# Second routed layer: token-major output projection with VectorE sums into x, and low parts of the scaled x from POOL

## The chip, the cores and the metric

One core of one Trainium2 chip runs the whole program. The metric is the device time in microseconds of one execution. The core's engines are TensorE (PE in the profile, with its weight loads as PEld), VectorE (DVE), ScalarE (ACT), POOL (GpSimd) and SyncE (SP), which issues the transfers. Each works through its own queue in order and waits on semaphores that the others raise.

## What is computed

The input x is 16 batches x 256 tokens x 128 features in float32. Four layers follow one another, each a cross-attention and a feed-forward part. The change is in the feed-forward part of the third of them, which routes tokens over 16 experts. It is the second of the two routed ones whose weights are loaded and split ahead in this way. Its reference, cut down:

```
n = layernorm(x)
w = gating(n)                      # softmax over the experts chosen, [tokens, 16]
q = sum_e w[:, e] * (n @ q_proj[e])      # k and v alike
a = softmax(causal(q @ k.T / sqrt(128))) @ v
x = x + sum_e w[:, e] * (a @ o_proj[e])
```

All products are to float32 accuracy.

## The kernel before

The tokens lie in x_sb as 32 tiles of 128; a block is four tiles (512 tokens, two batches), and there are ITERS = 8 blocks. `layer2_ffn` (L1588 on) writes the work of a block out by hand for each engine in a function `main(j, q)`. `run_mains` calls it for blocks 0 and 1, in a hardware loop for blocks 2 to 5, and for blocks 6 and 7. The order in which these functions issue is the order of each queue; nothing reorders it.

A block has two parts. **The q/k/v part** has a step per expert e. A selector product (`spread`, L1799) spreads the routing weights of expert e of all 512 tokens over the 128 partitions into a PSUM bank psR; VectorE multiplies the normalised x (xT, feature-major) by it (`scale_by`, L1980) into a ring of four, xs. ScalarE rounds that to xsh (L1727); VectorE subtracts, which gives the low part xsl (`low_part`, L1984). TensorE then adds nine products of rounded operands (low weight x high x, high x low, high x high, for q, k and v) to three PSUM banks (L1865). Expert 0 has three float32 products instead (L1860). The selector of step e+2 stands ahead of the products of step e. Between the steps stand the gate of the next block (`front_gate` to `front_parts`: some thirty small VectorE operations of 64 columns, after the scalings of e = 6, 7, 8, 9, 11 and 13) and its small products (after e = 2, 4 and 14).

**The part after it** has the attention of the block (scores, exponentials, transposes, `attend`) and, for the block before, the output projection `mix_o`: 16 steps, each a selector, a scaling of the attended values aoT by the same weights, and a float32 product with wo[e] into one bank psX (L1843). ScalarE copies the feature-major sum (L1722), four transposes turn it (L1793), and VectorE adds it to x (`add`, L2005) in the q/k/v part of two blocks later. POOL keeps a copy of the routes for that (L1681). `front_ln`, `front_xn` and `front_norm` prepare the normalised x of block j+2 there.

`layer2_ffn_weights` (L1571) lists what is loaded, copied and split for the layer while the attention ahead of it (`narrow_attention`) runs. The class `Ahead` (L110) does it: SyncE starts the loads in the first block of that attention, and POOL splits wq, wk and wv into high and low parts at its end (L134, L136).

The lines that decide the pace of a step, on TensorE:

```
pe.wait_ge(s("scaled").sem, s("scaled").at(n - 1))          # in spread
pe.wait_ge(s("x_split").sem, s("x_split").at(split_no(j, e) + 1))   # ahead of the nine products
```

and on VectorE:

```
dve.wait_ge(s("gate_bcast").sem, s("gate_bcast").at(n + 1))
dve.wait_ge(s("hidden").sem, s("hidden").at(n + 1 - RING))
```

## Time and profile before

| | |
|---|---|
| median of three runs | 2017.27 us (2017.11 to 2026.06) |
| the profiled execution | 2015.44 us, its span 2013.3 us |
| TensorE busy | 1626.2 us (81%), mean granted clock 0.899 of 2.4 GHz |
| TensorE weight loads busy | 1104.1 us (55%) |
| VectorE busy | 1284.4 us (64%) |
| ScalarE busy | 926.6 us (46%) |
| POOL busy | 210.0 us (10%) |

The layer that the change is in lies between about 1058 and 1613 us of the span. Busy times of TensorE come from records whose ends are modelled and which overlap, so the distance between starts is the better measure of what a product costs. The profile's views used here are the busy time of each engine by stretch, the timeline of one engine (start, duration, line, names, and in brackets the idle time ahead of it with what ended it), and the groups of like instructions with their mean duration.

### The profile page before, as it was taken

Reading aid. Unit: us, or ns where it says so; the run is one execution under the profiler, and the core shown is the slowest. Engines: PE = TensorE matmul, PEld = TensorE weight load, DVE = VectorE, ACT = ScalarE, POOL = GpSimd, SP = SyncE. Lnnn points to the kernel's source line nnn. Section 1 sums busy time; section 2 is a strip of 40 time slices with the busy share of each in tenths; the row PEclk is TensorE's granted clock in tenths of the full one; section 3 lists DMA queues with packets and bytes.
Section 4 is the critical chain, followed back from the end, with each engine's and each line's share of the span. In section 5 each row is a group of like instructions: output and inputs, shape, how many; then the busy total and the mean of one; then the engine's idle time right before and its main releaser. Section 6 shows DMA issues by size and latency. Waiting matters only on the chain. (4 is left out here: it accounts for less than half of the span.)

```text
span 2013.3 us, 27147 instructions
## 1 busy us (share of the span) xinstructions
PE 1626.2 (81%) x8633; PEld 1104.1 (55%) x8633; DVE 1284.4 (64%) x2870; ACT 926.6 (46%) x1759; POOL 210.0 (10%) x188
## 2 busy tenths in 40 slices
PE   6999938978869999978975899999999968848004
PEld 5777726855546666645653656656666445523004
DVE  4777771147657667646765566666665548776985
ACT  3555523356635565545551322222222146626862
POOL 2110020011200000011131000000000011010320
PEclk9999967959979999979996999999999969969557
DMA  4000000032100000023210000000000012100000
GB/s 149 1 1 0 0 1 0 0 112 47 39 1 0 1 0 0 1 91 104 60 26 0 1 1 0 1 1 0 0 1 0 0 50 50 43 0 0 0 0 42
DMA packets 23456, 41.71 MB, mean 21 GB/s; under 512 B 7720, under 2 KB 11184, under 8 KB 22320
## 3 DMA queue, kind: packets, MB, share of 16 engines
q1 hardware_dynamic: 23344, 40.32, 6.8%
q8 instruction: 58, 0.95, 0.2%
q14 instruction: 54, 0.44, 0.1%
HBM read 19.32 MB, written 2.10 MB: 11 GB/s over the span
## 5 line engine op out<-in xcount | busy, mean ns | idle before, releaser
L962 DVE TENSOR_REDUCE mP_a<-psY_a 128x8 f32<-128x512 f32 x192 | 128.2, 688 | 118.8 <-PE psY_a L800 117.9
L720 ACT ACTIVATE probs_a<-psX_a 128x512 f32<-128x512 f32 x192 | 109.1, 595 | 149.0 <-PE psX_a L827 148.3
L1727 ACT ACTIVATE xsh_f<-xs_f 128x512 fp32r<-128x512 f32 x120 | 75.8, 632 | 202.8 <-DVE xs_f L1980 202.6
L1980 DVE TENSOR_TENSOR xs_f<-xT_f,psR_f 128x512 f32<-128x512 f32 x128 | 86.9, 686 | 83.1 <-PE psR_f L1799 75.3
L1843 PE MATMUL psX_f<-xs_f,wo_f2w 128*128 128x512 f32 x256 | 128.6, 594 | 0.0
L2375 PE MATMUL ps_f<-wT_f,xq_f 128*128 128x128 f32 x192 | 24.5, 292 | 125.4 <-DVE xq_f L2396 125.4
L1980 DVE TENSOR_TENSOR xs_f<-aoT_f,psR_f 128x512 f32<-128x512 f32 x128 | 85.8, 685 | 61.6 <-PE psR_f L1799 61.4
L1507 DVE SCALAR_TENSOR_TENSOR g_f<-psU_f,cols_f1w,t_f 128x512 f32<-128x512 f32 (+1 forms) x104 | 77.9, 749 | 73.2 <-ACT t_f L1320 71.0
L800 PE MATMUL psY_a<-ks_a,xs_a 96*128 96x256 f32 x384 | 100.7, 367 | 28.0 <-DMA xs_a<-ql_a 16.3
L1402 PE MATMUL psO_f<-h_f,w_f1w 128*128 128x512 f32 (+1 forms) x208 | 107.6, 599 | 0.0
L1320 ACT ACTIVATE t_f<-psU_f,cols_f1w 128x512 f32<-128x512 f32 (+1 forms) x104 | 71.2, 684 | 76.0 <-PE psU_f L1386 76.0
L800 PEld LDWEIGHTS psY_a<-ks_a,xs_a 96*128 96x128 f32 x384 | 69.0, 215 | 59.6 <-issue 20.9
L827 PE MATMUL psX_a<-xs_a,ks_a 128*128 128x256 f32 x384 | 89.9, 336 | 10.2 <-ACT xs_a L712 10.2
L2375 PEld LDWEIGHTS ps_f<-wT_f,xq_f 128*128 128x128 f32 x192 | 23.8, 206 | 126.7 <-issue 126.7
L969 DVE RECIPROCAL heads_a<-psV_a 128x256 f32<-128x256 f32 x48 | 84.0, 1749 | 13.8 <-PE psV_a L840 13.8
L1984 DVE TENSOR_TENSOR xsl_f<-xs_f,xsh_f 128x512 fp32r<-128x512 f32 x120 | 82.5, 688 | 1.1
L827 PEld LDWEIGHTS psX_a<-xs_a,ks_a 128*128 128x128 f32 x384 | 66.8, 206 | 27.1 <-ACT xs_a L712 21.8
L1514 DVE TENSOR_TENSOR h_f<-act_h_f,psR_f 128x512 f32<-128x512 f32 (+1 forms) x104 | 70.5, 678 | 13.4 <-ACT act_h_f L1326 8.5
L179 POOL TENSOR_TENSOR rstd_f<-vareps_f,mhalf 128x4 f32<-128x4 f32 x16 | 16.2, 1010 | 580.1 <-DVE vareps_f L165 580.1
L376 ACT ACTIVATE vhat_a<-psF_a 64x256 f32<-64x256 f32 x122 | 46.1, 378 | 61.9 <-PE psF_a L434 61.1
L1865 PE MATMUL psQ_f<-xsh_f,wql_f2w 128*128 128x512 f32 x120 | 66.4, 554 | 5.0 <-DVE xsl_f L1984 4.9
L507 DVE TENSOR_REDUCE smax_a<-psS_a 128x16 f32<-128x1024 f32 x32 | 39.2, 1224 | 47.9 <-PE psS_a L441 47.9
(434 smaller groups left out, 4320.2 us busy)
## 6 DMA issues: line engine op xcount, KB each, us to landing
xs_a<-qh_a SPq DMA_DIRECT2D x192, 64.0 KB, 2.0
xs_a<-ql_a SPq DMA_DIRECT2D x96, 64.0 KB, 2.0
x_sb<-in_x SPq DMA_DIRECT2D x1, 2048.0 KB, 8.5
out<-x_sb SPq DMA_DIRECT2D x1, 2048.0 KB, 6.3
w_f1w<-in_F_w SPq DMA_DIRECT2D x2, 792.0 KB
ctxT<-in_ctxT SPq DMA_DIRECT2D x1, 1024.0 KB, 12.3
maskf_a<-in_mask SPq DMA_DIRECT2D x8, 128.0 KB, 2.3
maskf_a<-in_maskT SPq DMA_DIRECT2D x8, 128.0 KB, 2.5
```

The costliest lines, as they stand in the source:

```text
L720: nc.scalar.activation(probs[:, b % 2, g, :, :], psX[g % 2][:].rearrange("p (e t) -> p e t", e=2), ACT.Exp, scale=float(dv) ** -0.5).then_ ...
L800: ins = nc.tensor.matmul(psY[h % 2][:, e * GK:(e + 1) * GK], xs[0:MAXROW, j % 2, g, t:t + P], ks[0:MAXROW, j % 2, p, g, :], start=not mask ...
L827: ins = nc.tensor.matmul(psX[g % 2][:, e * ST:(e + 1) * ST], ks[:, j % 2, p, g, e * P:(e + 1) * P], xs[:, j % 2, g, p * ST:(p + 1) * ST], ...
L962: nc.vector.tensor_reduce(mP[:, b % 2, h // 2, col:col + 8], psY[h % 2][:].rearrange("p (h k) -> p h k", h=8), axis=AX.X, op=ALU.max).then ...
L969: nc.vector.reciprocal(heads[:, b % 2, :], psV[:, ST:2 * ST]).then_inc(s("sums_inverted").sem, 1)
L1320: nc.scalar.activation(t3[r, g % 2, :], psU[g % 2][r, 1, :], ACT.Identity, bias=cols[r, CH + g % CH:CH + g % CH + 1])\
L1402: ins = nc.tensor.matmul(psO[:], w2[0:rows[k], k, :], h[0:rows[k], g % 2, :], start=False, stop=k == CH - 1)
L1507: nc.vector.scalar_tensor_tensor(g_[r, g % 2, :], psU[g % 2][r, 0, :], cols[r, k:k + 1], t3[r, g % 2, :], ALU.add, ALU.mult).then_inc(s("h ...
L1727: nc.scalar.activation(xsh[:, e % RING, :], xs[:, e % RING, :], ACT.Copy).then_inc(s("x_high").sem, 1)
L1843: nc.tensor.matmul(psX[:], wo[:, e, :], xs[:, e % RING, :], start=e == 0, stop=e == E - 1)\
L1980: nc.vector.tensor_tensor(xs[:, e % RING, :], src, psR[e % 2][:], ALU.mult).then_inc(s("scaled").sem, 1)
L1984: nc.vector.tensor_tensor(xsl[:, e % RING, :], xs[:, e % RING, :], xsh[:, e % RING, :], ALU.subtract)\
```

## The change

**Output projection.** Instead of scaling the attended values by each expert's weights and adding in PSUM, the kernel multiplies the unscaled attended values, tokens as the stationary side, by the output weights of four experts at once: one group k of a block is tile c = k // 4 and experts 4g to 4g+3 with g = k % 4, 512 columns, in three rounded products (high and low halves aoh, aol of the attended values, and woh, wol of the weights). 16 groups a block alternate between two PSUM banks psO. VectorE adds the four results of a group to x, each times its column of the routing weights (`add_o`). Eight of the groups of block j-1 are multiplied in the q/k/v part of block j, after the steps 1, 3, ... 15; the other eight stand among the attention's products after it. The second selector product, the copies and the transposes go. The attended values' low half is made by VectorE (`attended_low`), which also keeps a copy of the routes.

**Low parts on POOL.** xsl comes from POOL, for all 16 experts; expert 0 has nine rounded products too.

**Smaller.** The selector of expert e is one column read 128 times, so that its table is 16 columns instead of 2048. The weights wq and wk are loaded into two raw buffers, split by POOL in the fifth block of the attention, and the buffers are then refilled with wv and wo (SyncE, in the seventh block), which POOL splits at the end; the first routed layer's split moves to the middle too. The score banks of the attention are packed in three banks instead of four, in the order 0, 2, 1, 3.

```diff
@@ class Ahead @@
+    def refill(self, pr, sp):
+        for k, pair in enumerate(self.refills):
+            sp.wait_ge(pr.sig("split").sem, pr.sig("split").at(2 * k + 2))
+            load(sp, pr.sig("refilled"), [pair])
...
-            pr.nc.gpsimd.tensor_tensor(lo, raw, hi, ALU.subtract)
+            pr.nc.gpsimd.tensor_tensor(lo, raw, hi, ALU.subtract).then_inc(pr.sig("split").sem, 1)
@@ narrow_attention @@
+                if j == ITERS - 2:
+                    ahead.refill(pr, sp)
...
-            ahead.split(pr, pool)
+                if j == ITERS // 2:
+                    ahead.split(pr, pool, 0)
+            ahead.split(pr, pool, 1)
@@ layer2_ffn, gpsimd @@
-            def keep_routes(j, q):
...
+            def low_part(j, e):
+                pool.wait_ge(s("x_high").sem, s("x_high").at(qn(j, e) + 1))
+                nc.gpsimd.tensor_tensor(xsl[:, e % RING, :], xs[:, e % RING, :], xsh[:, e % RING, :], ALU.subtract)\
+                    .then_inc(s("x_split").sem, 1)
             def main(j, q):
+                for e in range(E):
+                    low_part(j, e)
                 if has_second_next(j):
                     front(j + 2)
-                keep_routes(j, q)
@@ layer2_ffn, scalar @@
-                nc.scalar.activation(aoT[:, q, :], psM[:], ACT.Copy).then_inc(s("ao_ready").sem, 1)
+                if not is_first(j, 2):
+                    act.wait_ge(s("o_part").sem, s("o_part").at(OSTEPS * (j - 1)))
+                nc.scalar.activation(aoh[:, q, :], psM[:], ACT.Copy).then_inc(s("ao_high").sem, 1)
@@ layer2_ffn, tensor @@
-                nc.tensor.matmul(psR[e % 2][:], selb[:, e * P:(e + 1) * P], weights, start=True, stop=True)\
+                nc.tensor.matmul(psR[e % 2][:], selb[:, e:e + 1].broadcast_to([P, P]), weights, start=True, stop=True)\
...
+            def mix_o(j, q, k):
+                c, g = k // 4, k % 4
+                pe.wait_ge(s("o_steps").sem, s("o_steps").at(4 * (OSTEPS * j + k - 1)))
+                for m, (left, right) in enumerate(((aol, woh), (aoh, wol), (aoh, woh))):
+                    ins = nc.tensor.matmul(psO[k % 2][:], left[:, q, c * P:(c + 1) * P], right[:, 4 * g:4 * g + 4, :], start=m == 0, stop=m == 2)
+                ins.then_inc(s("o_part").sem, 1)
...
-                    if e == 10 and not is_first(j, 2):
-                        if not is_last(j):
-                            pe.wait_ge(s("gate_exp").sem, s("gate_exp").at(2 * j + 3))
-                        out_T(j - 2)
+                    if not is_first(j, 1) and e % 2 == 1:
+                        mix_o(j - 1, 1 - q, e // 2)
...
+                some_o(IN_LOOP, 10)
+                scores(j)
+                v_to_tokens(j)
+                some_o(10, 13)
+                probs_T(j, 0)
+                probs_T(j, 1)
+                some_o(13, 15)
+                probs_T(j, 2)
+                probs_T(j, 3)
+                some_o(15, OSTEPS)
+                attend(j)
@@ layer2_ffn, vector @@
+            def attended_low(j, q):
+                dve.wait_ge(s("ao_high").sem, s("ao_high").at(j + 1))
+                nc.vector.tensor_tensor(aol[:, q, :], psM[:], aoh[:, q, :], ALU.subtract).then_inc(s("ao_ready").sem, 1)
...
+            def add_o(j, k):
+                c, g = k // 4, k % 4
+                xc = x_sb[:, bass.ds(j * TPI + c, 1), :].rearrange("p a d -> p (a d)")
+                dve.wait_ge(s("routes_kept").sem, s("routes_kept").at(j + 1))
+                dve.wait_ge(s("o_part").sem, s("o_part").at(OSTEPS * j + k + 1))
+                for m in range(4):
+                    e = 4 * g + m
+                    dve.wait_ge(s("o_steps").sem, s("o_steps").at(4 * (OSTEPS * j + k) + m))
+                    nc.vector.scalar_tensor_tensor(xc, psO[k % 2][:, m * P:(m + 1) * P], routes_o[:, c, e:e + 1], xc, ALU.mult, ALU.add)\
+                        .then_inc(s("o_steps").sem, 1)
             def main(j, q):
                 for e in range(E):
                     scale_by(qn(j, e), e, xT[:, q, :])
-                    if e > 1:
-                        low_part(j, e - 1)
-                    if e == 12 and not is_first(j, 2):
-                        add(j - 2)
+                    if not is_first(j, 1) and e % 2 == 0 and e:
+                        add_o(j - 1, e // 2 - 1)
...
+                some_o(IN_LOOP - 1, 10)
+                maxima(j)
+                some_o(10, 11)
+                normalise(j, 0)
+                normalise(j, 1)
+                some_o(11, 12)
+                normalise(j, 2)
+                normalise(j, 3)
+                some_o(12, 14)
                 if has_second_next(j):
-                    stages.update({10: lambda: front_ln(j + 2), 12: lambda: front_xn(j + 2), 14: lambda: front_norm(j + 2)})
...
+                    front_ln(j + 2)
+                some_o(14, OSTEPS)
+                if has_second_next(j):
+                    front_xn(j + 2)
+                    front_norm(j + 2)
+                attended_low(j, q)
+                keep_routes(j, q)
```

How the change orders VectorE's queue at the start of a q/k/v part that carries sums (block 1). First the kernel before, in the same place of block 0, whose order there is that of all its blocks: L1980 scales, L1984 makes low parts, L1941 on is the gate.

```order
L1935 TENSOR_SCALAR ssq_f<-ssq_f 128x4
L1980 TENSOR_TENSOR xs_f<-xT_f,psR_f 128x512 x3
L1984 TENSOR_TENSOR xsl_f<-xs_f,xsh_f 128x512
L1980 TENSOR_TENSOR xs_f<-xT_f,psR_f 128x512
L1984 TENSOR_TENSOR xsl_f<-xs_f,xsh_f 128x512
L1980 TENSOR_TENSOR xs_f<-xT_f,psR_f 128x512
L1984 TENSOR_TENSOR xsl_f<-xs_f,xsh_f 128x512
L1980 TENSOR_TENSOR xs_f<-xT_f,psR_f 128x512
```

Now the change, block 1 (L1965 scales, L1999 is the sum of `add_o`, L1985 the attended values' low half):

```order
L1920 TENSOR_SCALAR ssq_f<-ssq_f 128x4
L1985 TENSOR_TENSOR aol_f<-psM_f,aoh_f 128x512
L1989 COPY routes_o_f<-routes_f 128x64
L1965 TENSOR_TENSOR xs_f<-xT_f,psR_f 128x512 x3
L1999 SCALAR_TENSOR_TENSOR x_sb<-psO_f,routes_o_f,x_sb 128x128 x4
L1965 TENSOR_TENSOR xs_f<-xT_f,psR_f 128x512 x2
L1999 SCALAR_TENSOR_TENSOR x_sb<-psO_f,routes_o_f,x_sb 128x128 x4
L1965 TENSOR_TENSOR xs_f<-xT_f,psR_f 128x512 x2
L1999 SCALAR_TENSOR_TENSOR x_sb<-psO_f,routes_o_f,x_sb 128x128 x4
L1926 TENSOR_TENSOR lg_f<-psM_f,rn_f 128x64
```

The low parts are gone from this queue; four sums stand after the scaling of every even expert from 2 on and ahead of that of the odd one behind it.

On TensorE, steps 1 and 2 of the same block in the change (L1849 the nine products, L1832 the output group, L1792 the selector):

```order
L1849 MATMUL psQ_f<-xsl_f,wvh_f2w 128x512
L1849 MATMUL psQ_f<-xsh_f,wvh_f2w 128x512
L1832 MATMUL psO_f<-woh_f2w,aol_f 128x512
L1832 MATMUL psO_f<-wol_f2w,aoh_f 128x512
L1832 MATMUL psO_f<-woh_f2w,aoh_f 128x512
L1792 MATMUL psR_f<-rwTb_f,selb_f2w 128x512
L1849 MATMUL psQ_f<-xsh_f,wql_f2w 128x512
L1849 MATMUL psQ_f<-xsl_f,wqh_f2w 128x512
```

The output group stands behind the products of the odd step and ahead of the selector and the products of the even one.

## Rows read from the trace of the kernel before

**Rows 1.** Busy by stretch: start:end, length, PE, PEld, DVE, ACT, POOL, PEclk, DMA, GB/s.

```profile
1080.00:1613.00 533.00, 503.02 (x2056) 325.51 (x2056) 329.31 (x792) 145.74 (x342) 23.11 (x22) 0.98 0.00 1
1270.20:1311.20 41.00, 40.13 (x176) 29.34 (x177) 25.66 (x62) 10.82 (x18) 0.00 (x0) 1.00 0.00 1
1311.20:1331.00 19.80, 18.88 (x76) 9.96 (x76) 14.81 (x41) 6.80 (x24) 1.01 (x1) 1.00 0.00 1
```

**Rows 2.** Timeline of TensorE, a steady block: start, us, instruction, idle before.

```profile
1268.98 0.59 PE L1799 MATMUL psR_f<-rwTb_f,selb_f2w 128*128 128x512 bf16 x2
1270.46 1.07 PE L1860 MATMUL psQ_f<-xs_f,wq_f2w 128*128 128x512 f32 x2
1273.08 0.38 PE L1799 MATMUL psR_f<-rwTb_f,selb_f2w 128*128 128x512 bf16 x1
1275.40 0.39 PE L1799 MATMUL psR_f<-rwTb_f,selb_f2w 128*128 128x512 bf16 x1
1311.17 0.61 PE L1799 MATMUL psR_f<-rwTo_f,selb_f2w 128*128 128x512 bf16 x2
1333.83 0.59 PE L1799 MATMUL psR_f<-rwTb_f,selb_f2w 128*128 128x512 bf16 x2
```

**Rows 3.** Timeline of TensorE: two output steps.

```profile
1329.97 0.38 PE L1799 MATMUL psR_f<-rwTo_f,selb_f2w 128*128 128x512 bf16 x1
1331.04 0.38 PE L1799 MATMUL psR_f<-rwTo_f,selb_f2w 128*128 128x512 bf16 x1
```

**Rows 4.** Timeline of VectorE, the same block.

```profile
1273.59 0.69 DVE L1980 TENSOR_TENSOR xs_f<-xT_f,psR_f 128x512 f32<-128x512 f32 x1 [1.42 <-PE psR_f L1799]
1283.81 0.23 DVE L1941 TENSOR_TENSOR lg_f<-psM_f,rn_f 128x64 f32<-128x64 f32 x1 [1.53 <-PE psM_f L1780]
1288.41 0.22 DVE L1951 TENSOR_REDUCE top_f<-gated_f 128x4 f32<-128x64 f32 x1
1289.12 0.22 DVE L1035 TENSOR_REDUCE gs_f<-lg_f 128x4 f32<-128x64 f32 x1
1289.37 0.22 DVE L1036 TENSOR_TENSOR tmp_f<-lg_f,gs_f 128x64 f32<-128x64 f32 x1
1290.58 0.69 DVE L1980 TENSOR_TENSOR xs_f<-xT_f,psR_f 128x512 f32<-128x512 f32 x1 [0.21 <-DVE oh_f L1039]
```

**Rows 5.** Timelines of VectorE and ScalarE: one scaling and its rounding.

```profile
1300.50 0.68 DVE L1980 TENSOR_TENSOR xs_f<-xT_f,psR_f 128x512 f32<-128x512 f32 x1
1301.21 0.63 ACT L1727 ACTIVATE xsh_f<-xs_f 128x512 fp32r<-128x512 f32 x1 [2.49 <-DVE xs_f L1980]
```

**Rows 6.** Groups by line: count | busy us, mean ns | idle before.

```profile
L2401 DVE SCALAR_TENSOR_TENSOR x_sb<-ps_f,scale_f,x_sb 128x512 f32 x6 | 4.5, 751 | 5.0 <-PE ps_f L2375 4.8
L533 DVE TENSOR_TENSOR x_sb<-x_sb,psC_a 128x128 f32<-128x128 f32 x16 | 4.5, 283 | 7.8 <-PE psC_a L456 7.7
L2005 DVE TENSOR_TENSOR x_sb<-x_sb,psM_f 128x512 f32<-128x512 f32 x4 | 2.8, 688 | 9.3 <-PE psM_f L1793 9.3
L331 POOL TENSOR_TENSOR cbl_a<-cb_a,cbh_a 128x256 fp32r<-128x256 f32 x8 | 5.9, 740 | 1.2 <-POOL cbh_a L328 0.2
L136 POOL TENSOR_TENSOR wkl_f2w<-wk_f2w,wkh_f2w 128x2048 fp32r<-128x2048 f32 x1 | 4.6, 4629 | 0.1
```

**Rows 7.** Timeline of VectorE, preparing the block after next.

```profile
1328.93 1.11 DVE L171 TENSOR_SCALAR xn_f<-x_sb,mean_f,rstd_f 128x128 f32 x4
1331.38 0.17 DVE L1935 TENSOR_SCALAR ssq_f<-ssq_f 128x4 f32<-128x4 f32 x1 [0.15 <-ACT sq_f L1701]
```

**Rows 8.** Busy time by stretch, start of the second block (columns as rows 1).

```profile
1139.00:1145.00 6.00, 5.92 (x9) 2.56 (x10) 2.09 (x4) 1.26 (x2) 1.65 (x2) 0.51 0.01 3
```

**Rows 9.** Timeline of TensorE in the attention before.

```profile
916.18 0.61 PE L794 MATMUL psY_a<-maskb_a,identb 128*128 128x512 bf16 x1 [4.63 <-DMA xs_a<-ql_a]
```

**Rows 10.** Timeline of VectorE, first scaling and last sum of the layer.

```profile
1083.47 2.08 DVE L1980 TENSOR_TENSOR xs_f<-xT_f,psR_f 128x512 f32<-128x512 f32 x3
1612.09 0.69 DVE L2005 TENSOR_TENSOR x_sb<-x_sb,psM_f 128x512 f32<-128x512 f32 x1 [3.36 <-PE psM_f L1793]
```

More of the change, by code:

```diff
@@ L1636, in qn @@
         def qn(j, e):
[L1637 to L1644 removed]
+            return E * j + e
         def run_mains(eng, main):
@@ L1968, in front_weights, with front_parts @@
                 steps.done(nc.vector.reciprocal(gs[:], gs[:]))
[L1969 to L1972 removed]
+                steps.done(nc.vector.tensor_tensor(routes[:, q, :, :], ex[:], gs[:].unsqueeze(2).broadcast_to(g4), ALU.mult))
+            def front_parts(steps, q):
+                three_parts(nc, steps, routes[:, q, :, :], parts[:], hi[:], rest[:], mid[:], E).then_inc(s("gate_ready").sem, 1)
                 steps.n += 2
```

244 lines of the change are left out of this document (93 added, 151 removed).

## Prediction

> **What bounds the kernel now.** I read the busy time by stretches first. In the second routed layer (1080 to 1613 us of the span) TensorE is nearly always at work: 40.13 of 41.00 us in the part of a block that makes q, k and v, 18.88 of 19.80 in the part after it [rows 1]; VectorE has 25.66 and 14.81 us there. The TensorE timeline of one steady block gives the beats [rows 2]: the q/k/v part begins at 1270.46, is over at 1311.17 (40.7 us), and the next block's selectors follow at 1333.83. Block to block is 1268.98 to 1333.83, 64.85 us. One expert's step is 2.32 us (1273.08 to 1275.40: one selector matmul and nine products, 0.23 us each). In the second part an output step costs 1.07 us [rows 3]. So TensorE bounds this layer, and VectorE runs up to two steps ahead of it. That lead is what hides the path of an expert's step: scale on VectorE, round on ScalarE, low part, products.
>
> **What the change takes off TensorE.** Per block: 16 output steps of 1.07 us become 16 groups of three rounded products, 3 x 0.23 = 0.70 us each, -5.9 us; the transposes back of the output go (about 0.4, half of a float32 product below); three float32 products of the first step (1270.46 to 1273.08, 2.6 us [rows 2]) become nine rounded ones, 2.1 us. Together -6.9 us per block, 55 us in eight. It counts only where TensorE still ends the wait.
>
> **What it adds, part by part.**
> *Sums.* A block gets 64 VectorE sums of 128x128, PSUM times a column plus x. The same form with 512 columns took 751 ns; a column costs (688 - 283) / 384 = 1.05 ns [rows 6], so 128 columns take about 0.35 us. Each waits on the one before it. Chained operations of 0.22 us start 0.25 us apart (1289.12 and 1289.37 [rows 4]), 0.035 after the end of the one before, so a chained sum comes every 0.386 us. Unchained ones overlap: four normalisations of 0.34 us take 1.11 together, one per 0.26 [rows 7]. A group of four followed by an unchained operation is 3 x 0.386 + 0.26 = 1.42 us, a group followed by another group 1.54. Bounds for one sum: 0.26 (no price for the chain) and, in the four looped blocks, the 0.21 us of register work seen before the scaling at 1290.58 [rows 4] once per group, +13 us in all.
> *Low part on POOL.* It took 740 ns for 256 columns and 4629 for 2048 [rows 6]: 2.17 ns a column, 1.30 us for 512. Bounds 1.11 (slope alone) and 1.48 (twice 256). Against 2.32 us per step POOL keeps up; its rate costs nothing, its latency does.
> *The wait that decides.* VectorE's queue in a q/k/v part is now: scale(e), the four sums of group e/2 - 1 for even e, scale(e+1). That group's product stands on TensorE behind the nine products of step e-1. So the sums can't start before TensorE is at step e, and scale(e+1) queues behind them: the lead of two steps is gone. From the start of step e's products: the group's last product started 0.47 us earlier, and a VectorE operation starts 0.51 us after its producer starts (1273.08 to 1273.59 [rows 2, 4]), so 0.04; sums 1.42; scale to round 0.71 (1300.50 to 1301.21 [rows 5]); round 0.63 + 0.05; low part 1.30 + 0.04. That is 4.19 us until step e+1 can start, where 2.32 are needed: **TensorE stands 1.87 us at each of seven odd steps**. Step 7 waits 0.74 longer, for four small gate operations between the sums and its scaling (the first 0.23 at 1283.81, the others taken at 0.17 like the small one of [rows 7]), and step 9 waits 2.17 longer, for the second-best search (1288.41 to 1290.58 [rows 4]). The small transposes and gate products of the part vanish in these stalls. Its length: 16 x 2.1 + 13 selectors x 0.23 = 36.6, seven groups of products 4.9, stalls 13.1 + 2.9 = **57.5 us where 40.7 stood**, +16.8. The last block has no gate work, +13.9. Seven blocks carry sums (the first has none): 6 x 16.8 + 13.9 = +114.7.
> *After the q/k/v part* two PSUM banks alternate, so products follow VectorE. VectorE: 0.95 until group 7 is there, nine groups x 1.54 = 13.9, its other work 5.2 (the 14.81 us of 41 operations less 15 scalings at 0.64, where some adjoin [rows 1]), the wait for the squares 1.35 (from the normalisation at 1328.93 to 1331.38, less its own 1.11 [rows 7]), low half and copy of the routes 0.8, and then a full hand-off to the next block's first step, 2.8: 25.0 us, against 1311.17 to the first product of the next block, 24.1. Five times +1.0; block 6 has nothing to prepare for a block 8, -4.1 on VectorE, which TensorE before couldn't use: -3.2. Sum +1.8.
> *The ends.* The first block starts 1.6 us later (hand-off) and pays low half, copy and hand-off again at its end: +3 net of its cheaper first step. The last block: 18.3 us to the low half, then sixteen groups x 1.54 = 24.7 and 1.0 to the first, 44.0, against 1311.17's counterpart to the last sum, 44.9: -1.
> *The clock.* After idle TensorE is granted 1.2 GHz: about half the clock over the 6 us with which the second block begins [rows 8], some 5.5 us of them work, costing half of that. Steady blocks had none of it. Now TensorE stands about 8 us before every block (its last product waits for nothing more than VectorE's long queue), +2.7 us x 6 (the first restart was there before), and 4 us before step 9; I take 1.5 us there, six times. With the last block's half share: +25. Bounds: 0, and the whole layer at the low level (a rival).
> *Covered or small.* Weight splits on POOL now sit in the middle and at the end of the attention before; the subtraction alone is 4.63 us each [rows 6]. POOL has nothing else to do in those stretches but the next statistics, which are needed half a tile group later; with that cover gone each split would cost its own time. In that attention 3 MB less are loaded while the mask is fetched; TensorE stood 4.63 us there for a transfer [rows 9]: -5. A selector now is one column read 128 times; no row has such a load. Below nothing; above one product, 0.23 x 128 x half of the steps (the others stand anyway) = +15. I take nothing, since a plain selector load hides.
>
> **Sum:** 3 + 114.7 + 1.8 - 1 + 25 - 5 = +139 us on this layer's 529.3 (1083.47 to the last sum's end at 1612.78 [rows 10]). The profiled execution took 2015.44 us (span 2013.3): 2154. The median of the three runs shown is 1.8 us above it, so **2156 us, 7% slower**.
>
> **A rule against the price of the chain.** The rows say that a chained operation costs 0.13 us more than an unchained one [rows 4, 7]. The Trainium skill (VectorE: DVE Perf Modes, The DRAIN you can't avoid) says that a semaphore after each operation costs nothing extra, eight copies having taken 13.88 us either way. By that rule the sum comes 58 us lower, as worked out under rival 2; the rows decide for me.
>
> **Rivals.**
> 1. *TensorE's saving wins* (faster). Place: odd steps of the q/k/v part. -6.9 us x 8 and -5 of the attention: **1957**. It decides where a stall is under 6.9 / 7 = 1.0 us, so where the next scaled x is ready 3.3 us after the sums can begin. Of these the hand-off without any sum takes 2.73, so four sums would have to fit in 0.6 us; four of the cheapest operations of that size take 1.04. For it: VectorE is busy only 25.66 of 41.00 us [rows 1]. Against: the order of its queue, which no average shows. 5%.
> 2. *Chained sums cost what unchained ones do.* 147 chained sums inside the q/k/v parts and 316 after them, 463 x 0.126 = 58 us less: **2098**. For it: nothing but that the chained pair seen is of small operations. 10%.
> 3. *The clock stays at 1.2 GHz.* A pair of steps has 23 products; at 0.43 us each it is 9.8 instead of 7.2 us, 18 us per block, if in most blocks: **2260**. For it: the gaps of 1.9 us in every 7.2; against: a slow TensorE has no gaps, and the second block, which begins slow [rows 8], ran at full clock after it: the layer's mean is 0.98 [rows 1]. 6%.
> 4. *The change doesn't do what it says* (the order of the queues differs in the looped blocks, no stall, no gain): **2017**. The printed order shows all blocks alike. 2%.
>
> **How the numbers follow.** My forecast has 77%. Its own terms (sum price -58, POOL -11/+10, registers +13, selector +15, clock -25/+30) seldom all fall on one side. The range, 2090 to 2220, takes in rival 2 and leaves out rivals 1, 3, 4 (13%) and a rest. About 0.5% (10 us) is what a measurement of this kernel can tell from no change. Faster: rival 1, 5%. Same: rival 4 and a coincidence, 3%. Slower: 92%.
>
> **What would show it.** Right: 512 sums with a mean of 0.35 us; 128 low parts on POOL of about 1.3 us; TensorE idle before the products of odd steps some 1.9 us, released by POOL; a steady block of about 86 us; VectorE idle for the output product just before the sums at even steps; clock near 0.9 over the layer. Wrong: no wait of products on POOL's low part; sums starting while TensorE is a step behind; blocks near 58 us; the attention before it longer than now.

## The result and the profile after

| | before | changed |
|---|---|---|
| median | 2017.66 us (4 runs, 2017.11 to 2026.06) | 2202.45 us (4 runs, 2194.59 to 2206.09) |
| ratio | | 1.0900, 95% interval 1.0859 to 1.0941 |
| profiled execution, span | 2015.44, 2013.3 us | 2194.59, 2192.6 us |
| first product to last sum of the layer | 1084.62 to 1612.78, 528.2 us | 1091.39 to 1787.61, 696.2 us |
| what follows the layer | 400.5 us | 405.0 us |

The change makes the kernel 9.0% slower; the forecast was 2156 us in a range of 2090 to 2220. From the profile page of the changed kernel, its busy line and three groups (count | busy us, mean ns of one | idle time before them and what ended it):

```profile
PE 1639.4 (75%) x8575; PEld 1149.7 (52%) x8625; DVE 1324.5 (60%) x3142; ACT 920.5 (42%) x1759; POOL 369.5 (17%) x310
...
L1999 DVE SCALAR_TENSOR_TENSOR x_sb<-psO_f,routes_o_f,x_sb 128x128 f32<-128x128 f32 (+1 forms) x512 | 179.4, 350 | 291.3 <-PE psO_f L1832 214.3
...
L1690 POOL TENSOR_TENSOR xsl_f<-xs_f,xsh_f 128x512 fp32r<-128x512 f32 x128 | 162.0, 1277 | 343.5 <-ACT xsh_f L1728 343.5
...
L1849 PE MATMUL psQ_f<-xsh_f,wql_f2w 128*128 128x512 f32 x128 | 73.8, 576 | 89.7 <-POOL xsl_f L1690 89.7
```

Both new prices are as forecast: a sum 0.350 us, a low part 1.28. VectorE stood 214 us for the output products, and TensorE stood 89.7 us for POOL's low parts, which is the wait that was to show. By stretches (columns as in [rows 1]): the layer, the q/k/v part of the fourth block and the part after it (the one beside which the hardware loop returns, 3 us longer than the others), and the two parts of the last block, which has no gate work:

```profile
1088.50:1787.70 699.20, 514.26 (x2017) 369.24 (x2046) 358.05 (x1060) 140.01 (x333) 175.10 (x141) 0.90 0.00 1
1325.80:1390.90 65.10, 51.17 (x192) 37.42 (x196) 25.67 (x72) 9.27 (x17) 19.03 (x16) 0.89 0.00 1
1390.90:1419.00 28.10, 15.19 (x63) 10.72 (x63) 20.43 (x68) 8.38 (x28) 3.21 (x3) 0.80 0.01 1
1684.90:1740.80 55.90, 43.71 (x177) 31.42 (x180) 17.56 (x41) 8.00 (x13) 18.74 (x15) 1.00 0.00 0
1740.80:1787.60 46.80, 30.85 (x110) 19.05 (x108) 38.19 (x114) 5.59 (x17) 0.00 (x0) 0.89 0.00 1
```

In [rows 1] TensorE worked 40.13 of 41.00 us and VectorE 25.66. Now VectorE does the same work in that part (25.67) and TensorE somewhat more (51.17: output groups are new in it, and some of it runs at the lower clock), but in 65.1 us. Neither is the bound: they wait for each other. The TensorE timeline of that block shows where (the first product of steps 2, 3, 4, 7, 8, 9 and 10, and the selectors ahead of 7 and 9):

```profile
1333.62 0.58 PE L1849 MATMUL psQ_f<-xsh_f,wql_f2w 128*128 128x512 f32 x1
1338.15 0.49 PE L1849 MATMUL psQ_f<-xsh_f,wql_f2w 128*128 128x512 f32 x1 [1.42 <-POOL xsl_f L1690]
1341.08 0.59 PE L1849 MATMUL psQ_f<-xsh_f,wql_f2w 128*128 128x512 f32 x1
...
1351.61 0.39 PE L1792 MATMUL psR_f<-rwTb_f,selb_f2w 128*128 128x512 bf16 x1 [0.70 <-DVE xs_f L1965]
1353.61 0.49 PE L1849 MATMUL psQ_f<-xsh_f,wql_f2w 128*128 128x512 f32 x1 [1.61 <-POOL xsl_f L1690]
1356.62 0.51 PE L1849 MATMUL psQ_f<-xsh_f,wql_f2w 128*128 128x512 f32 x1
1361.14 0.39 PE L1792 MATMUL psR_f<-rwTb_f,selb_f2w 128*128 128x512 bf16 x1 [2.14 <-DVE xs_f L1965]
1363.15 0.80 PE L1849 MATMUL psQ_f<-xsh_f,wql_f2w 128*128 128x512 f32 x1 [1.61 <-POOL xsl_f L1690]
1368.53 0.72 PE L1849 MATMUL psQ_f<-xsh_f,wql_f2w 128*128 128x512 f32 x1
```

Steps 2 to 3 are 4.53 us apart, 3 to 4 are 2.93. The hand-off between the first two can be read link by link from VectorE, ScalarE and POOL:

```profile
1333.99 1.51 DVE L1999 SCALAR_TENSOR_TENSOR x_sb<-psO_f,routes_o_f,x_sb 128x128 f32 x4 [8.90 <-PE psO_f L1832]
1335.41 1.27 DVE L1965 TENSOR_TENSOR xs_f<-xT_f,psR_f 128x512 f32<-128x512 f32 x2
...
1341.36 1.51 DVE L1999 SCALAR_TENSOR_TENSOR x_sb<-psO_f,routes_o_f,x_sb 128x128 f32 x4 [4.67 <-PE psO_f L1832]
```

```profile
1336.13 1.22 ACT L1728 ACTIVATE xsh_f<-xs_f 128x512 fp32r<-128x512 f32 x2 [10.38 <-DVE xs_f L1965]
```

```profile
1336.83 2.51 POOL L1690 TENSOR_TENSOR xsl_f<-xs_f,xsh_f 128x512 fp32r<-128x512 f32 x2 [8.52 <-ACT xsh_f L1728]
```

From the first product of step 2: sums after 0.37, scaling 1.42 later, rounding 0.72, low part 0.70, products 1.32: 4.53 us. VectorE was idle for 4.67 us ahead of the next sums. It had time, but its next instruction was one that TensorE could not yet release.

### The profile page after: what moved, and what is told of

The parts are those of the page before. It is cut to its first block and busy times, and to the rows that moved or that the text cites. A ratio compares the mean times of both kernels' runs of the same rounds, so it can differ in the third digit from the quotient of the medians.

```text
span 2192.6 us, 27697 instructions
## 1 busy us (share of the span) xinstructions
PE 1639.4 (75%) x8575; PEld 1149.7 (52%) x8625; DVE 1324.5 (60%) x3142; ACT 920.5 (42%) x1759; POOL 369.5 (17%) x310
## 5 line engine op out<-in xcount | busy, mean ns | idle before, releaser
L1999 DVE SCALAR_TENSOR_TENSOR x_sb<-psO_f,routes_o_f,x_sb 128x128 f32<-128x128 f32 (+1 forms) x512 | 179.4, 350 | 291.3 <-PE psO_f L1832 214.3
L1690 POOL TENSOR_TENSOR xsl_f<-xs_f,xsh_f 128x512 fp32r<-128x512 f32 x128 | 162.0, 1277 | 343.5 <-ACT xsh_f L1728 343.5
L1849 PE MATMUL psQ_f<-xsh_f,wql_f2w 128*128 128x512 f32 x128 | 73.8, 576 | 89.7 <-POOL xsl_f L1690 89.7
L2370 PE MATMUL ps_f<-wT_f,xq_f 128*128 128x128 f32 x192 | 24.8, 295 | 126.7 <-DVE xq_f L2391 126.7
L1965 DVE TENSOR_TENSOR xs_f<-xT_f,psR_f 128x512 f32<-128x512 f32 x128 | 84.9, 681 | 20.8 <-PE psR_f L1792 13.8
L1832 PE MATMUL psO_f<-woh_f2w,aol_f 128*128 128x512 f32 x128 | 63.3, 495 | 40.2 <-DVE x_sb L1999 38.5
L1849 PEld LDWEIGHTS psQ_f<-xsh_f,wql_f2w 128*128 128x128 f32 x128 | 27.4, 214 | 106.8 <-POOL xsl_f L1690 98.5
L1792 PE MATMUL psR_f<-rwTb_f,selb_f2w 128*128 128x512 bf16 x98 | 41.5, 424 | 53.7 <-DVE xs_f L1965 52.0
```

The lines of the kernel that those rows point to most:

```text
L1690: nc.gpsimd.tensor_tensor(xsl[:, e % RING, :], xs[:, e % RING, :], xsh[:, e % RING, :], ALU.subtract)\
L1849: ins = nc.tensor.matmul(psQKV[n][:], wp[:, e, :], xp[:, r, :], start=e == 0 and m == 0, stop=e == E - 1 and m == 2)
L1965: nc.vector.tensor_tensor(xs[:, e % RING, :], src, psR[e % 2][:], ALU.mult).then_inc(s("scaled").sem, 1)
L1999: nc.vector.scalar_tensor_tensor(xc, psO[k % 2][:, m * P:(m + 1) * P], routes_o[:, c, e:e + 1], xc, ALU.mult, ALU.add)\
```

## Experiments

All kernels are variants of the changed one. "Layer" is from the first product of its first step to the end of its last sum, in the profiled execution.

| kernel | median us | starts at | layer us |
|---|---|---|---|
| before | 2017 to 2020 | 1084.6 | 528.2 |
| changed | 2202.5 | 1091.4 | 696.2 |
| sums_behind | 2078.6 | 1094.6 | 582.6 |
| lows_on_dve | 2304.9 | 1096.0 | 801.7 |
| behind_lows_dve | 2110.4 | 1096.0 | 614.0 |
| sums_free (one run) | 2136.7 | 1097.5 | 636.8 |
| splits_apart (one run) | 2192.5 | 1088.4 | 699.5 |
| warm | 2179.0 | 1102.4 | 676.4 |
| early_scales | 2071.7 | 1099.1 | 570.5 |
| more_in_loop | 2047.7 | 1096.7 | 541.5 |
| low_half_first | 2011.9 | 1086.1 | 524.9 |
| x_later | 2013.0 | 1084.8 | 523.2 |
| thirteen_in_loop | 2011.8 | 1084.3 | 521.2 |

### The sums behind the next scaling

```diff
-                    if not is_first(j, 1) and e % 2 == 0 and e:
+                    if not is_first(j, 1) and e % 2 == 1 and e > 1:
                         add_o(j - 1, e // 2 - 1)
```

Only the place of the sums in VectorE's queue moves, by one scaling.

> One thing moves against the changed kernel (2202 us): on VectorE the four sums of group k stand behind the scaling of expert 2k+3, no longer ahead of it. Queue theory (the sums wait for a product on TensorE and hold back the next scaling): the next scaling that queues behind the sums is that of step 2k+4, which is needed only after two whole steps, 5.3 us; its hand-off is 4.4 us, so TensorE no longer stands at plain odd steps, and only the gate's searches leave 1 to 2 us a block. The part that makes q, k and v falls from 65 to about 44 us in six blocks and from 56 to 39 in the last: some 140 us less, about 2060. The part after it stays at 25 us. Rival A (POOL's low parts set the pace, 1.28 us each behind the rounding): the stalls stay, released by POOL, and the time stays within 2 per cent of 2200. Rival B (half of the loss is TensorE's slow clock in whatever order): the stalls go but the granted clock stays near 0.88, about 2110.

Measured: 2078.60 us, ratio to before 1.0306 (1.0264 to 1.0348), 124 us less than the change. Steps 2 to 5 of the last block in this kernel, TensorE and then VectorE:

```profile
1595.43 0.58 PE L1849 MATMUL psQ_f<-xsh_f,wql_f2w 128*128 128x512 f32 x1
1597.76 0.58 PE L1849 MATMUL psQ_f<-xsh_f,wql_f2w 128*128 128x512 f32 x1
1600.79 0.58 PE L1849 MATMUL psQ_f<-xsh_f,wql_f2w 128*128 128x512 f32 x1
1603.11 0.58 PE L1849 MATMUL psQ_f<-xsh_f,wql_f2w 128*128 128x512 f32 x1
```

```profile
1601.00 1.51 DVE L1999 SCALAR_TENSOR_TENSOR x_sb<-psO_f,routes_o_f,x_sb 128x128 f32<-128x128 f32 x4 [2.16 <-PE psO_f L1832]
1602.43 0.68 DVE L1965 TENSOR_TENSOR xs_f<-xT_f,psR_f 128x512 f32<-128x512 f32 x1
```

The same sums wait for the same product (0.21 us after step 4 starts), but the scaling behind them at 1602.43 is that of step 6, not of step 5. A pair of steps takes 5.36 us, which is TensorE's own work, instead of 7.32. The last q/k/v part went from 55.9 to 41.7 us, a steady one from about 65 to 48. What is left above the expected 44 in a steady one is the gate's searches and slow products behind the 25 us tail; the last one has neither, so the expected 39 was less than TensorE's own work. POOL's rate as the limit (rival A) is out, and so is rival B: the granted clock of a steady q/k/v part rose from 0.89 to 0.96, and the time is 31 us below its 2110.

### Low parts on VectorE, with the sums ahead and with the sums behind

```diff
-                for e in range(E):
-                    low_part(j, e)
...
                 for e in range(E):
                     scale_by(qn(j, e), e, xT[:, q, :])
+                    if e:
+                        low_part(j, e - 1)
```

(The removed lines are POOL's; low_part(j, E - 1) follows VectorE's loop.)

> The changed kernel (2202 us) with the 128 low parts back on VectorE, each behind the next scaling as in the kernel before; the sums keep their place ahead of the odd scalings. Queue theory: the hand-off at an odd step is sums 1.43, scaling 0.6, the next scaling 0.6 (which hides the rounding), low part 0.7 where POOL took 1.28: 4.38 becomes about 3.9 to 4.0 us, so 0.4 x 7 x 7 = 20 us less, and VectorE operations are no longer stretched to over 1 us beside a POOL one: 2175 to 2185. Rival (moving the low parts to POOL is what lost the time): well under 2100, most of the stalls gone. Rival on the other side (VectorE is short of time): slower than 2210, since VectorE gets 11 us of work more in each block and the low part of step e can only follow the next scaling.

Measured: 2304.88 us, 1.1428 (1.1391 to 1.1465). My number was 125 us off, and the rival on the other side came true: I had looked at odd steps alone. TensorE, first products of steps 10, 11 and 12 of the fourth block, and VectorE ahead of step 10:

```profile
1413.98 0.50 PE L1842 MATMUL psQ_f<-xsh_f,wql_f2w 128*128 128x512 f32 x1 [2.87 <-DVE xsl_f L1962]
1417.36 0.98 PE L1842 MATMUL psQ_f<-xsh_f,wql_f2w 128*128 128x512 f32 x1
1423.92 0.50 PE L1842 MATMUL psQ_f<-xsh_f,wql_f2w 128*128 128x512 f32 x1 [2.75 <-DVE xsl_f L1962]
```

```profile
1411.22 1.51 DVE L1997 SCALAR_TENSOR_TENSOR x_sb<-psO_f,routes_o_f,x_sb 128x128 f32 x4 [5.61 <-PE psO_f L1825]
1412.65 0.68 DVE L1958 TENSOR_TENSOR xs_f<-xT_f,psR_f 128x512 f32<-128x512 f32 x1
1413.24 0.69 DVE L1962 TENSOR_TENSOR xsl_f<-xs_f,xsh_f 128x512 fp32r<-128x512 f32 x1
```

The low part of the even step 10 (1413.24) stands behind the sums, and these wait for the group that TensorE multiplies just ahead of step 10. So the even step has no lead at all: sums 1.43, scaling 0.6, low part 0.7, TensorE idle for 2.87. This pair takes 9.9 us. With the sums in this place, having the low parts on POOL thus saves 102 us of stall. Whether they are worth as much in the better order:

> The kernel with the sums behind the next scaling (2079 us) with the low parts on VectorE, each behind the next scaling. Tells what POOL's low parts are worth once the sums stand well. Queue theory: the low part of step 2k+3 now stands behind the sums of group k, which can't start before step 2k+2: ready 0.37 + 1.43 + 0.6 + 0.7 = 3.1 us after that start, where the step is due 2.3 us after it: 0.8 us of stall per pair and 2 to 3 us at the searches: 2125 to 2150. Rival A (the order alone mattered): within 10 us of 2079. Rival B (POOL's low parts are always worth the 100 us that they were worth with the sums ahead): about 2180.

Measured: 2110.42 us, 1.0465 (1.0435 to 1.0495); 32 us above the same order with POOL, a little under my range, and far from either rival. In the last block, every other step waits 0.29 us for the low part and a pair takes 5.91 us (1631.91 to 1637.82) instead of 5.36:

```profile
1631.91 0.50 PE L1842 MATMUL psQ_f<-xsh_f,wql_f2w 128*128 128x512 f32 x1 [0.29 <-DVE xsl_f L1962]
1634.85 0.59 PE L1842 MATMUL psQ_f<-xsh_f,wql_f2w 128*128 128x512 f32 x1
```

The two parts of the change don't add: POOL's low parts are worth 102 us with the sums in the bad place and 32 with them in a better one.

### What a chained sum costs

```diff
-                    dve.wait_ge(s("o_steps").sem, s("o_steps").at(4 * (OSTEPS * j + k) + m))
-                    nc.vector.scalar_tensor_tensor(xc, psO[k % 2][:, m * P:(m + 1) * P], routes_o[:, c, e:e + 1], xc, ALU.mult, ALU.add)\
+                    dve.wait_ge(s("o_steps").sem, s("o_steps").at(4 * (OSTEPS * j + k) + m - 3))
+                    nc.vector.scalar_tensor_tensor(acc[:, m, :], psO[k % 2][:, m * P:(m + 1) * P], routes_o[:, c, e:e + 1], xc, ALU.mult, ALU.add)\
```

This kernel leaves out the update of x by the layer's output projection.

> The 512 sums go into four scratch tiles of 128 columns, one for each expert of a group, and none waits for the one just ahead of it (only for the one four back), so x isn't updated by this layer's output projection; the waits for the group's product and all places in the queue stay. Measures the price of the chain. My price (0.387 apart chained, 0.26 unchained): four sums take 1.13 instead of 1.51 us; 0.38 x 7 x 7 in the part that makes q, k and v, 0.5 x 9 x 8 in the parts after it: 50 to 55 us less, about 2145. Rule theory (a semaphore on the one ahead costs nothing, the spacing is that of the operation): the spacing stays at 0.387 and the time within 5 us of the changed kernel.

Measured, in one run: 2136.72 us against the 2194.59 of the changed kernel's profiled execution, 58 less; the layer alone 59.4 less. By its steps some 50 of these are the chain's: 4.00 instead of 4.38 us at a plain odd step (19 us in 49 of them), 3.1 to 4.2 us in each of six gaps between q/k/v parts, 10.6 at the end of the last block. The other 9 came with fewer slow products. Four sums and the scalings behind them:

```profile
1415.57 1.13 DVE L2000 SCALAR_TENSOR_TENSOR acc_f<-psO_f,routes_o_f,x_sb 128x128 f32<-128x128 f32 x4 [4.67 <-PE psO_f L1833]
1416.62 1.27 DVE L1966 TENSOR_TENSOR xs_f<-xT_f,psR_f 128x512 f32<-128x512 f32 x2
```

Four unchained sums take 1.13 us, one every (1.13 - 0.35) / 3 = 0.26; chained they took 1.51, one every 0.387. The prediction had 0.26 and 0.386, from other operations of [rows 4, 7]. The rule of the Trainium skill (VectorE: DVE Perf Modes, The DRAIN you can't avoid), by which a semaphore after each operation costs nothing, doesn't hold for these 128-column sums: a wait on the one just ahead costs 0.13 us each. The run takes away that wait and the dependence on its result together (each of four sums has a tile of its own), so it doesn't tell one from the other.

### POOL's splits in two tile groups

```diff
-                if j == ITERS // 2:
-                    ahead.split(pr, pool, 0)
+                if j in (ITERS // 2 - 1, ITERS // 2):
+                    ahead.split(pr, pool, 0, j - ITERS // 2 + 1)
```

(Each call splits one of the two weights.) In the changed kernel, the attention before the layer has this on POOL, and this wait on TensorE:

```profile
942.71 1.28 POOL L676 TENSOR_TENSOR x_sb<-x_sb,bo_a2w 128x512 f32<-128x512 f32 x1 [10.22 <-DVE xn_a L184]
943.93 1.89 POOL L147 CAST wqh_f2w<-raw_f2w 128x2048 fp32r<-128x2048 f32 x1
945.90 4.55 POOL L149 TENSOR_TENSOR wql_f2w<-raw_f2w,wqh_f2w 128x2048 fp32r<-128x2048 f32 x1
950.40 1.89 POOL L147 CAST wkh_f2w<-raw_f2w 128x2048 fp32r<-128x2048 f32 x1
952.36 4.49 POOL L149 TENSOR_TENSOR wkl_f2w<-raw_f2w,wkh_f2w 128x2048 fp32r<-128x2048 f32 x1
957.22 1.14 POOL L192 TENSOR_TENSOR rstd_a<-vareps_a,mhalf 128x4 f32<-128x4 f32 x1 [0.36 <-DVE vareps_a L178]
```

```profile
957.75 0.59 PE L811 MATMUL psY_a<-maskb_a,identb 128*128 128x512 bf16 x1 [6.67 <-DVE maskb_a L952]
```

Four operations, 12.9 us, stand ahead of the statistics that VectorE needs for the next tile group.

> In the attention ahead of the layer POOL makes the two weight splits after the fourth and after the fifth tile group, one each (6.4 us), instead of both after the fifth (12.9 us). Cover theory: the space between POOL's bias addition and the next statistics is about 6.3 us, so both hide but for 0.2 us, TensorE's wait of 6.67 us near 957 us falls to 1.3, and the layer starts 5 us earlier; the whole is 5 us shorter (2190 against 2195 of the profiled execution). Rival (the transfers or the scores in three banks delay that attention): the layer starts where it does now, 1088.5 us, and the wait only moves.

Measured: the wait is gone, and the statistics follow on time:

```profile
952.37 0.38 PE L812 MATMUL psY_a<-maskb_a,identb 128*128 128x512 bf16 x1 [1.29 <-DVE maskb_a L953]
```

By its first product the layer started at 1088.4, 3.0 us earlier and not 5. (The 1088.5 of the expected text is where the changed kernel's stretch above begins, ahead of its first product at 1091.4.) The three tile groups from 931.88 on took 20.5 us each at a granted clock of 0.92; in the kernel before they took 18.9 at 1.00. The other kernels bear out the split: from POOL's first instruction of that attention to the layer's first product, the eight kernels with both splits together took 216.9 to 220.5 us, the four with the splits apart 209.5 to 214.2, and the kernel before 209.4. A single run of 2192.5 us can't show 5 us in the whole.

### TensorE kept at work in its stalls

```diff
+            def warm(n, q, fresh=False):
+                for _ in range(n):
+                    nc.tensor.matmul(psQKV[0][:], zero[:], rwTb[:, q, :], start=fresh, stop=fresh)
...
+                    warm(16, q, True)
...
+                        warm(2 if e not in (7, 9) else 4 if e == 7 else 10, q)
...
+                        warm(6, q)
```

> The changed kernel (2202 us) with TensorE kept at work in its stalls: products of a zero tile that add nothing (16 ahead of the second selector of a block, 2 to 10 ahead of the selector in an odd step from 3 on, 6 ahead of the nine products of these). The order of all else, and so every stall, stays. Clock theory (about 5 us of each of six blocks are products at 1.2 GHz after a stall: steps 1, 2 and 10 took 4.1, 3.6 and 5.4 us where the last block has 2.2, 3.0 and 2.9): the granted clock of the steady blocks rises from 0.88 to 1.00 and the time falls by 25 to 35 us, to about 2172; the queue alone then accounts for the rest. Rival A (the slow stretches lie beside VectorE's waits and cost nothing): clock 1.00, time within 8 us of 2202. Rival B (the added products come late and delay the real ones): slower than 2210.

Measured: 2179.03 us, 1.0784 (1.0759 to 1.0808), 23 us less (25 to 35 were expected), with 82 more products in a block and every real instruction in its place. The fifth block's two parts, in the changed kernel and then in this one:

```profile
1419.10:1485.00 65.90, 52.17 (x192) 37.83 (x196) 25.49 (x72) 9.35 (x17) 18.91 (x15) 0.89 0.00 0
1485.00:1509.90 24.90, 14.92 (x63) 10.55 (x63) 20.30 (x68) 8.72 (x28) 3.30 (x4) 0.84 0.00 0
```

```profile
1418.40:1481.10 62.70, 61.82 (x261) 41.10 (x262) 25.49 (x72) 9.24 (x16) 19.00 (x15) 0.95 0.00 0
1481.10:1506.00 24.90, 16.10 (x81) 10.26 (x79) 20.28 (x68) 8.62 (x28) 3.25 (x3) 1.00 0.00 0
```

The clock is worth 3.2 us in this q/k/v part (2.3 to 5.7 in the others) and nothing in the part after it, which VectorE sets: 24.9 us at a clock of 0.84 and of 1.00. Summed over the second to the seventh block the gain is 21 us; the clock was not at 1.00 throughout and the added products can themselves delay a step, so this is a lower bound for what the low clock costs, beside the forecast's 25.

### Towards a version that keeps the saving

Each of these kernels holds the edits of the ones ahead of it, sums_behind's first; only the main lines are shown. The first two scalings of the next block, with their rounding and low parts, move ahead of the end of the tail (the part after q/k/v):

```diff
+                if not is_last(j):
+                    spread(qn(j + 1, 0), 0, rwTb[:, 1 - q, :])
+                    spread(qn(j + 1, 1), 1, rwTb[:, 1 - q, :])
                 some_o(15, OSTEPS)
                 attend(j)
...
+                next_scale(0)
                 some_o(13, 14)
                 if has_second_next(j):
                     front_ln(j + 2)
+                next_scale(1)
```

> The kernel with the sums behind the next scaling (2079 us), and besides the scalings of experts 0 and 1 of the next block, with their rounding and low parts, moved ahead of the last sums, of the normalised x and of the attended values' low half; their selectors stand ahead of the last output group. Theory: the 7 us in which TensorE stands ahead of a block are VectorE's queue plus one full hand-off; with the first two steps ready only VectorE's work from the last sum on is hidden behind two steps of products: 6 to 7 us less in each of seven blocks, and the slow clock of steps 0 and 1 (2.5 us a block) goes with it: about 60 us less, 2015 to 2025, level with the kernel before. Rival (VectorE is short of time over the whole block, 47 of 73 us busy, so the work only moves): the stall comes back at steps 2 to 4, and less than 25 us are won.

Measured: 2071.66 us, 1.0254 (1.0227 to 1.0281), 7 us less than sums_behind, not 60: the rival's size, with the stall a little earlier than it said. The gap between the parts fell from 25 to 21 us, but steps 0 and 1 grew, since TensorE then stood behind step 0 (2.8 and 4.0 us in two blocks) for the attended values' low half, still the second last instruction of VectorE's tail.

Then eleven groups in the first part, and the gate one to two steps earlier (PROD lists the steps behind which a group stands; a group's sums stand two scalings later):

```diff
-        IN_LOOP = 8
+        PROD = (1, 3, 5, 7, 9, 10, 11, 12, 13, 14, 15)
+        IN_LOOP = len(PROD)
```

> As the kernel with early scalings, but eleven of the sixteen output groups stand in the part that makes q, k and v (behind steps 1, 3, 5, 7, 9, 10, 11, 12, 13, 14, 15), their sums two scalings later, and the gate's pieces come one to two steps earlier, so that no pair of steps has more than one search beside its sums. Theory: with five groups instead of eight in the tail, VectorE's part of it is 4.6 us shorter, and TensorE has 2.1 us more in the first part: 2.5 us less per block in the tail and 3 us less of gate stalls in steps 8 to 10: 58 to 61 us a block against 64.85 before the change, 1975 to 1995 in all, faster than both kernels. Rival (sums every step starve the scalings): stalls at steps 11 to 15 released by POOL, and the time is above that of the kernel with early scalings.

Measured: 2047.69 us, 1.0141 (1.0119 to 1.0163). 24 us less, but the blocks took 65.1 to 69.4 us, above the expected 58 to 61. Steps 11 to 15 came every 3.03 us without a stall, so the sums don't starve the scalings; what was left was 3.9 us behind step 0 for the low half and 1.2 in step 7.

```diff
-                some_o(14, OSTEPS)
+                some_o(14, 15)
+                attended_low(j, q)
+                some_o(15, OSTEPS)
                 if has_second_next(j):
                     front_xn(j + 2)
                     front_norm(j + 2)
-                attended_low(j, q)
```

> As the kernel with eleven groups in the first part (2048 us), and: the attended values' low half ahead of the last sums and of the normalised x, the first two normalisations ahead of a group of sums, the group behind step 5 moved behind step 6 and that of 7 behind 8, and POOL's two splits of the attention before in different tile groups. Theory: TensorE's wait of 3.9 us behind step 0 (for that low half, behind seven VectorE operations) and of 1.2 us in step 7 go, and 1 to 2 us of the tail: 68.4 us a block become about 62.5, 6 us in six or seven blocks, and 3 to 5 us in the attention: 2005 to 2012, some 0.5 per cent faster than the kernel before or level with it. Rival (VectorE, 46 of 68 us busy, is the bound through its waits): the stall moves to steps 2 to 4 and under 15 us are won.

Measured: 2011.90 us (12 runs, 2006.55 to 2018.11), 0.9976 (0.9961 to 0.9990): as expected, and the first that isn't slower than before. Several edits went in at once, so the 36 us that it gained are not shown to be the low half's. In the profiled executions 10.7 us are the earlier start of the layer (the weight splits are apart now, and 2.5 us come from ahead of that attention), and 16.6 are the layer's.

Two more: one has the transposes of the next normalised x, the first pieces of the gate and the wait for the low half a step later and the groups in other places, the other thirteen groups besides.

> As the kernel with the low half first (2012 us, 64.6 us a block), with the transposes of the next block's normalised x behind step 1 instead of step 0, the gate's first three pieces one step later, the wait for the attended values' low half behind step 1, and the eleven groups behind steps 1, 2, 3, 7, 8 and 10 to 15. Theory: TensorE's wait of 1.6 to 2.1 us behind step 0 (for a normalised x that VectorE makes last in the tail) and the slow products that follow it go, and the searches stand where no sums do: 61 to 62 us a block, 3 us in seven blocks, 1985 to 1995, over 1 per cent faster than the kernel before. Rival (VectorE's waits only move): above 2005.

> The same with thirteen groups in the first part (behind steps 1, 2, 3 and 6 to 15) and three in the tail. Theory: the tail's waits for a free bank (three of 0.5 to 1.1 us a block, ended by sums) go, and TensorE has 1.4 us more in the first part and 1.4 less in the tail: 1 to 2 us a block less than with eleven, 1975 to 1990. Rival (VectorE at steps 8 to 13 has 2.1 us of scaling and sums plus the gate's 1.1 against TensorE's 3.0): stalls released by POOL appear there and it is no faster than with eleven.

Measured: 2012.97 us, 0.9990 (0.9972 to 1.0009), and 2011.75 us, 0.9971 (0.9956 to 0.9986). The expected 20 to 30 us didn't come: the stall moved from step 0 to step 2, which is x_later's rival. Thirteen groups made the layer 2.0 us shorter than eleven, in one profiled execution each; the medians can't be told apart. TensorE and VectorE at the start of a block of the last kernel:

```profile
1400.40 0.39 PE L1809 MATMUL psR_f<-rwTb_f,selb_f2w 128*128 128x512 bf16 x1 [1.36 <-DVE xs_f L1986]
1402.40 0.79 PE L1863 MATMUL psQ_f<-xsh_f,wql_f2w 128*128 128x512 f32 x1 [1.61 <-POOL xsl_f L1695]
```

```profile
1396.89 1.11 DVE L185 TENSOR_SCALAR xn_f<-x_sb,mean_f,rstd_f 128x128 f32 x4
1399.35 0.17 DVE L1941 TENSOR_SCALAR ssq_f<-ssq_f 128x4 f32<-128x4 f32 x1 [1.34 <-ACT sq_f L1719]
1399.45 0.20 DVE L2010 COPY routes_o_f<-routes_f 128x64 f32<-128x64 f32 x1
1399.65 1.28 DVE L1986 TENSOR_TENSOR xs_f<-xT_f,psR_f 128x512 f32<-128x512 f32 x2
```

The scaling of step 2 (1399.65) stands behind the normalisation and a wait of 1.34 us for ScalarE's squares. It is the same fault for the third time; moving that scaling ahead of them wasn't tried. thirteen_in_loop's layer is 7.0 us shorter than before's (521.2 against 528.2), and its whole profiled execution 6.0: what stands ahead of the layer and behind it takes nearly the same (1084.3 and 401.8 us against 1084.6 and 400.5).

## Why the prediction was right, and where it was short

The side, the mechanism and its place were right: +139 us forecast, +179 measured in the profiled executions (185 between the medians). Four of the five terms came out above the forecast and the fifth about level; the prediction had held it rare that its terms all err to one side, and its range was just wide enough. By the terms of the sum:

| | forecast | measured |
|---|---|---|
| up to the first step's products | -5 + 1.6 | +6.8 |
| first block | +1.4 | +1.0 |
| blocks 1 to 6, clock included | +128 | +146.8 |
| last block | +13 | +20.3 |
| behind the layer | 0 | +4.5 |

**The wait that decides.** Forecast 4.19 us for the hand-off, measured 4.53 beside step 2 of a steady block and 4.38 in the last one, whose pairs take 7.32 us with the clock at 1.00. All links were within 0.03 but the first: the sums start 0.22 (last block) to 0.37 us (step 2 of the steady one) after the step's first product, where I had 0.04. I had put the group's last product 0.47 us ahead of the step's first, two spacings of a product; the selector between them starts 0.04 us ahead of the product, and the distance is 0.28 (1333.34 to 1333.62). Beside step 2 the sums also started 0.65 us behind that last product, not 0.51 (0.54 beside step 4). By the whole hand-off, 4.38 to 4.53 for 4.19, seven times in seven blocks that is 9 to 17 us. The sums_behind run shows that this queue position, not POOL's rate, is the bulk of the loss (124 of 185 us).

**The gate's two long steps** were right: 0.77 more at step 7 (forecast 0.74) and 2.15 at step 9 (2.17), from 5.15 and 6.53 against 4.38 us.

**The clock.** Right in kind and nearly in size. Behind the two long waits of the steady block shown (ahead of step 0 and of step 9) TensorE was granted 1.2 GHz: products 0.43 us apart from 1363.74 to 1368.01, so that step 9 to 10 took 5.38 us where the last block has 2.93. Mean 0.90 over the layer. The fourth, sixth and seventh block are like that. In the second, third and fifth the low clock also came behind step 7's wait, and steps 7 to 8 and 9 to 10 took 4.5 us each; in two of them it came behind step 11's wait of 1.6 us as well. Against the last block's steps a block lost 4.5 to 6.5 us, where the forecast had 4.2; of these the restarts beside the gate, costed at 1.5, took 2.4 to 4.6. Blocks took 88 to 93 us (the seventh 85), about 86 being the forecast.

**The part after q/k/v.** 24.8 to 25.2 us between the parts, forecast 25.0. One gap, where the hardware loop returns, was 28.3 (before it was 25.6 against 24.0), which no term had. Behind the seventh block it was 22.1, where the forecast comes to 20.9.

**The last block** was mis-sized by its baseline: I took 40.7 us for its q/k/v part before, but without gate products that part took 37.7. Its measured length of 55.9 was forecast at 54.6. Its end took 46.8 us for 44.0.

**The attention before it** is the step that failed. The prediction said of the weight splits that "POOL has nothing else to do in those stretches but the next statistics, which are needed half a tile group later", and gave the relief of a transfer, -5. The relief came (4.63 us of [rows 9] became 1.6), but two splits are 12.9 us of POOL, where it had been idle for 7.9 ahead of those statistics: they came late, and TensorE stood 6.67 us instead of 1.29. The condition was named and its length not added up (two subtractions of 4.6 and two casts of 1.9). splits_apart removed that wait. Its 5.4 us more are a part of the 10.2 us that this line of the table is off. The tile group with the wait had a granted clock of 0.84 and the next one 0.87, and together they took 9.2 us more than two groups in the kernel before (25.87 and 21.16 against 18.9 each).

**Rivals.** The saving on TensorE (rival 1) can be seen in its piece, a group of 0.69 us (1332.89 to 1333.58) for an output step of 1.07, but it was small beside the waits: of 55 us forecast for eight blocks, the best of the later kernels shows 7.0 in its layer. Rival 2 gave 58 us for unchained sums, and sums_free measured 58, so the row of [rows 4] was the right one to choose; that the two numbers are the same is in part luck, since some 9 us of the measured ones are the clock's. Rival 3: in the q/k/v parts the clock fell only behind waits of 1.6 us and more, and not behind each of those, and it came back within about a dozen products.

## What to carry to other kernels

In an in-order queue the place of an instruction that waits matters more than its length: before putting one in, name what is queued behind it and how many steps ahead of need that is; groups of four sums, 1.4 us each, cost 124 us one place too early. An offload to another engine has no price of its own: the same low parts on POOL were worth 102 us in one order and 32 in another. Where a long job is slipped into an idle stretch, add up the whole job against that stretch, and look at what the next small instruction on that engine is for.

## What the hardware showed that was not expected

**VectorE held beside POOL.** In the changed kernel one or two 128x64 operations of a block, most of them with two SBUF inputs, take five times their time (0.22 us otherwise):

```profile
1352.49 1.15 DVE L1056 TENSOR_TENSOR oh_f<-desc_f2w,gs_f 128x64 f32<-128x64 f32 x1
```

```profile
1352.30 1.26 POOL L1690 TENSOR_TENSOR xsl_f<-xs_f,xsh_f 128x512 fp32r<-128x512 f32 x1 [5.59 <-ACT xsh_f L1728]
```

It ends at 1353.64, 0.08 us after POOL's low part does. Ten such operations of 0.7 us and more stand between 1150 and 1600 us (eight with two SBUF inputs, two casts with one), eighteen in sums_behind, and none in the kernel before or in lows_on_dve, where POOL makes no low parts; scalings, which read PSUM too, keep their length beside POOL (0.69 us at 1362.44). That agrees with the Trainium skill (SBUF — State Buffer, SBUF: two separate sides), which has VectorE and POOL share a pair of ports under a lock that one instruction holds to its end. It cost little here: in this block step 7 to 8 took 3.01 us, where the last block has 2.94. In a queue without slack it would be 0.9 us a time, which is an estimate (1.15 less 0.22).

**The clock of an unchanged stage moves.** Eight kernels with the same program ahead of the layer started it between 1091.4 and 1102.4 us. Up to 8.8 us of that were there when the attention ahead of the layer began (873.6 to 882.4; the stretch from 300 to 600 us has a granted clock of 0.83 to 0.87 in them). That attention's tile groups take 18.9 us at a granted clock of 1.00 and 20.5 at 0.92. The attention behind the layer did likewise: up to its fifth statistics it took 60.3 us at 0.60 in the changed kernel and 56.8 at 0.70 in the kernel before, which is 3.5 of the 4.5 us there. What tips it wasn't found. A difference of under 10 us between two of these kernels is better read from the layer's own length than from the whole.
